# Up matmuls two tiles ahead of the down matmuls in three stretches of a routed feed-forward, attention, feed-forward kernel

## The reference

```python
x = L0_attn_x                                  # (32, 256, 128) float32, 8192 tokens of 128
x = x + 0.5 * ffn(layernorm(x), Wg, bg, W1, b1, W2, b2)
x = x + attn(layernorm(x), Wq, Wk, Wv, Wo)
x = x + 0.5 * ffn(layernorm(x), Wg, bg, W1, b1, W2, b2)

def ffn(x):                                    # 8 experts, hidden 512, the best 2 of each token
    probs, idx = top_k(softmax(x @ Wg + bg), 2)
    h = gelu(einsum('nd,edh->enh', x, W1) + b1)
    eo = einsum('enh,ehd->end', h, W2) + b2
    return einsum('nk,nkd->nd', probs, eo[idx])

def attn(x):                                   # 16 heads of 8 channels
    each token attends to itself and the 8 tokens before it
```

## Time and profile before

| what | value |
|---|---|
| median of 3 runs | 1040.05 us (1038.57 to 1041.2) |
| span of the profiled execution | 1184.4 us, 144.35 above the median; no other time of that execution is listed |
| PE busy | 883.4 us, 75% of the span |
| POOL busy | 665.5 us, 56% |
| DVE busy | 645.4 us, 54% |
| ACT busy | 501.1 us, 42% |
| mean granted clock of TensorE | 0.897 of full speed |

### The profile page before, as it was taken

The page is one execution under the profiler, slowest core; times in us unless marked ns, Lnnn a source line. Parts: engine busy times, 40 slices in busy tenths (PEclk is TensorE's granted clock), DMA queues, the critical chain, the costliest instruction groups (busy, mean ns, idle before and its releaser), DMA issues.

```text
span 1184.4 us, 22517 instructions
## 1 busy us (share of the span) xinstructions
PE 883.4 (75%) x6345; PEld 759.1 (64%) x6345; DVE 645.4 (54%) x1309; ACT 501.1 (42%) x1215; POOL 665.5 (56%) x593
## 2 busy tenths in 40 slices
PE   3347757576987789996999659897875766975983
PEld 3336647475866677785778545686765655864873
DVE  5774132431357688896989998686851411210222
ACT  4434424243623373744545325644342333422432
POOL 2574445545678666345677456356763545455552
PEclk9998859887989899998999978998986977987997
DMA  8314212262214421144112121422221224532683
GB/s 261 110 58 96 53 41 56 70 161 61 59 51 115 110 51 39 26 119 99 33 47 47 48 79 45 78 55 59 56 59 44 50 59 104 134 87 64 155 195 119
DMA packets 170488, 96.44 MB, mean 81 GB/s; under 512 B 137712, under 2 KB 154406, under 8 KB 169604
## 3 DMA queue, kind: packets, MB, share of 16 engines
q1 hardware_dynamic: 152420, 59.29, 21.7%
q0 software_dynamic: 17952, 35.71, 9.8%
HBM read 25.77 MB, written 52.35 MB: 66 GB/s over the span
## 4 chain that ended last, share of the span: by engine, by line
PE 40%; DVE 16%; issue 15%; another core or an unknown queue 14%; ACT 5%; DMA 4%; POOL 3%; SPq 3%; ACTq 0%; DVEq 0%; POOLq 0%
PE bank L979 16%; PE bank L962 11%; PE bank L877 3%; POOL x_sorted L591 3%; ACT h_f L766 2%; DVE prod L1167 2%; DVE prod L1178 2%; PE bank L850 2%; DMA x_sorted<-hl,slots_all 2%; DVE y_sb L1432 2%; PE bank L864 2%; PE bank L973 1%; DVE prod L1213 1%; PE bank L803 1%
## 5 line engine op out<-in xcount | busy, mean ns | idle before, releaser
L605 POOL DMA_INDIRECT y_pairs<-y_sb,tile_ids x305 | 355.1, 1164 | 329.5 <-issue 256.1
L766 ACT ACTIVATE h_f<-bank,b_cols 128x256 f32<-128x256 f32 (+1 forms) x736 | 266.0, 440 | 434.8 <-PE bank L962 242.6
L591 POOL DMA_INDIRECT x_sorted<-hl,slots_all x256 | 301.8, 1179 | 174.3 <-issue 87.0
L979 PE MATMUL bank<-w_sb,h_f 128*128 x2440 | 346.1, 295 | 20.8 <-issue 12.3
L979 PEld LDWEIGHTS bank<-w_sb,h_f 128*128 128x128 f32 x2440 | 317.6, 207 | 29.0 <-issue 24.7
L962 PE MATMUL bank<-xsT,w_hl 128*128 128x256 f16 (+1 forms) x2208 | 262.6, 269 | 59.1 <-ACT h_f L766 25.7
L962 PEld LDWEIGHTS bank<-xsT,w_hl 128*128 x2208 | 199.6, 104 | 97.1 <-issue 70.8
L1432 DVE TENSOR_TENSOR y_sb<-bank,tile_ids 128x256 f32<-128x256 f32 (+1 forms) x184 | 68.8, 375 | 328.5 <-PE bank L979 179.2
L973 PE MATMUL bank<-b_hl,ones_b 128*128 x184 | 49.8, 270 | 85.5 <-DVE y_sb L1432 69.7
L973 PEld LDWEIGHTS bank<-b_hl,ones_b 128*128 128x128 f16 x184 | 18.6, 101 | 104.7 <-issue 101.8
L1213 DVE TENSOR_TENSOR prod<-score,qkv 128x2304 f32<-128x2304 f32 x32 | 81.7, 2552 | 0.2
(11 more groups left out here) (159 smaller groups left out, 849.8 us busy)
## 6 DMA issues: line engine op xcount, KB each, us to landing
y_in<-y_pairs SPq DMA_DIRECT2D x28, 512.0 KB
x_sorted<-no_rows SPq DMA_DIRECT2D x7, 720.0 KB
y_pairs<-y_sb,tile_ids POOLq DMA_INDIRECT x305
x_sorted<-hl,slots_all POOLq DMA_INDIRECT x256
x_sorted<-no_rows SPq DMA_DIRECT2D x56, 72.0 KB
x_sb<-in_L_attn_x SPq DMA_DIRECT2D x3, 1024.0 KB, 6.4
out<-x_sb SPq DMA_DIRECT2D x3, 1024.0 KB
xsT<-x_sorted SPq DMA_TRANSPOSE x184
```

What stands on the lines that cost most here:

```text
L591: pool.indirect_dma_start(out=x_sorted[p], out_offset=bass.IndirectOffsetOnAxis(ap=slots_all[:, at:at + 1], axis=0), in_=hl[:, c % 2, i // ...
L605: pool.indirect_dma_start(out=y_pairs, out_offset=bass.IndirectOffsetOnAxis(ap=tile_ids[:, t.n % IDS, i, 0:1].bitcast(U32), axis=0), in_=y ...
L766: ins = act.activation(h_part(t, b)[:, k, :], bank[h_banks.uses[u][0]][:, k * t.slots:(k + 1) * t.slots], ACT.Gelu, bias=b1_cols[:, bass.d ...
L979: ins = pe.matmul(into[:, half, :], h_part(t, c // t.per)[:, c % t.per, half * P:(half + 1) * P], w2_flat[:, bass.ds((e * HC + c) * D, D)] ...
```

## The change

PE orders `up` and `down` anew in three stretches, banks are dealt anew, and group 3's turned tokens use one bank.

- The stages are cut elsewhere: stage 0 is part 0 and the first 8 tiles of part 1 (tiles 0 to 31), stage 2 begins at tile 24 of part 4 (tiles 120 to 183).
- In stages 0 and 2 `down` stands two tiles behind `up`; in stage 1 one tile, as before. At the end of a part all downs that are left come before the next part's first `up`.
- Up matmuls get bank 4 in stage 0 beside 0, 1 and 2, and tiles 120 to 159 go from banks (0, 1) to (0, 1, 2, 6). Down matmuls of tiles 120 to 159 go from bank 3 alone to (3, 7, 4), those of tiles 24 to 31 from bank 3 to (3, 7), and part 6 gets bank 4 as a third one.
- Since bank 4 is taken, all four quads of group 3 are turned in bank 5, each behind the copy of the one before.
- Two new waits on PE: tile 0 waits until the quads of groups 0 to 2 are copied, tile 120 until attention has been added in all groups and the last keys and values are copied.

```diff
+EARLY_END = (1, 8)
+LATE_BEGIN = (4, 24)
+AHEAD = (2, 1, 2)
@@ class Tile
-        self.stage = 0 if p == 0 else 2 if p == len(n_wide) - 1 else 1
+        self.stage = 0 if (p, at) < EARLY_END else 2 if (p, at) >= LATE_BEGIN else 1
+        self.ahead = AHEAD[self.stage]
@@ banks
-        h_banks, y_banks = Banks((0, 1, 2), (0, 1), (0, 1, 2, 6)), Banks((3, 7), (3,), (3, 7))
+        h_banks, y_banks = Banks((0, 1, 2, 4), (0, 1), (0, 1, 2, 6)), Banks((3, 7), (3,), (3, 7, 4))
+        def quad_bank(q, i):
+            return bank[5] if q == G - 1 else bank[4 + i % 2]
@@ ACT, copy_turned: reads quad_bank(q, i) in place of bank[4 + i % 2]
@@ PE, turn_quad
                 if n >= 2:
-                    pe.wait_ge(quads_ready, n - 1)
+                    pe.wait_ge(quads_ready, n if q == G - 1 else n - 1)
@@ PE, experts
-                earlier_tile = None
+                behind = []
                 for t in ALL_TILES:
-                    if t.begins_late:
-                        yield from down(*earlier_tile)
+                    while t.begins_late and behind:
+                        yield from down(*behind.pop(0))
...
                     e = of_these[t.at % LOADS]
+                    if t.n == 0:
+                        pe.wait_ge(quads_ready, (G - 1) * QUADS)
+                    if (t.p, t.at) == LATE_BEGIN:
+                        pe.wait_ge(attn_added, G * CH)
+                        pe.wait_ge(qkv_ready, G * KV)
                     yield from up(t, e)
-                    if earlier_tile and not t.begins_late:
-                        yield from down(*earlier_tile)
-                    earlier_tile = (t, e)
-                yield from down(*earlier_tile)
+                    behind.append((t, e))
+                    while len(behind) > t.ahead:
+                        yield from down(*behind.pop(0))
+                while behind:
+                    yield from down(*behind.pop(0))
```

More of the change, by code:

```diff
@@ L662, in copy_turned @@
                         act.wait_ge(quads_turned, q * QUADS + i + 1)
-                        act.copy(xnT_p[:, 4 * i:4 * i + 4, HALO:HALO + P], bank[4 + i % 2][:].rearrange("p (j n) -> p j n", n=P)
+                        act.copy(xnT_p[:, 4 * i:4 * i + 4, HALO:HALO + P], quad_bank(q, i)[:].rearrange("p (j n) -> p j n", n=P)
                                  ).then_inc(quads_ready, 1)
@@ L791, in turn_quad @@
                 if n >= 2:
-                    pe.wait_ge(quads_ready, n - 1)
+                    pe.wait_ge(quads_ready, n if q == G - 1 else n - 1)
                 for j in range(4):
-                    ins = pe.transpose(bank[4 + i % 2][:, j * P:(j + 1) * P], xn_at[q][:, 4 * i + j, :], ident[:])
+                    ins = pe.transpose(quad_bank(q, i)[:, j * P:(j + 1) * P], xn_at[q][:, 4 * i + j, :], ident[:])
                 ins.then_inc(quads_turned, 1)
```

## The result

The changed kernel takes **1047.0 us** (median of 7, 1044.16 to 1049.27), the kernel before beside it 1038.57 (median of 7, 1032.8 to 1042.1): ratio 1.008, 95% interval 1.0052 to 1.0108. It is slower by 0.8%, where 0.8% faster was forecast, and lies above the range's 1044. The granted clock isn't the difference: its mean over the seven runs is 0.931 of full speed for the changed kernel, and 0.931 over 26 runs of the kernel before.

The account below looks back on a forecast made before the run. No engine was full over the whole span; what counts is where PE, the busiest, is held. 1.6 + 0.6 - 1.7 - 4.1 - 3.2 - 1.0 = -7.8 us gave 1032, range 1022 to 1044.

Parts of the forecast that it names:

- Moved past: Stages 0 and 2: each `down` one `up` later (1.47 or 0.88 us) may delay DVE's `take_y`; counted 0.
- Starts of parts: PE at part starts: +1.1 and -1.2 us, cancelling for parts 5 and 6; +0.6 at tile 0, 0 for part 1.
- Rival 2: Slower: later results delay POOL's rows at parts 1 and 6, plus 1.1 at four starts; +6.1 us, 1046; chance 0.17.
- Waits taken away: PE's bank waits removed: part 1's head -1.7 us, part 4 -4.1, part 5 -3.2, part 6 -1.0.
- slowed stretches: Some 25 stretches of about 10 us with PE and SP slowed together, taken as profile recording, absent from timed runs.
- rival 1: POOL's scatters between results 135 and 153 hold part 6, so little changes: 1038 us; chance 0.33.
- Quads: Group 3's turned quads on PE: second waits for first's copy, 0.8 us for each of two pairs, +1.6.
- The new waits: PE's waits at tiles 0 and 120, for copies and additions expected to be done already: 0 us.
- Rival 3: Much faster: slowed stretches also occur in timed runs, a third of 69.7 us counts: 1018 us; chance 0.08.
- what would show it: Signs: PE's `y_sb` waits after tile 120 near 0 confirm banks; more PE idle before a part's first tiles refutes the forecast.

Follow-up runs that it names:

- a1: Changed kernel with `down` one tile behind `up` everywhere, keeping its banks, single quad bank and new waits; 1040.07 us, ratio 1.0005 to the kernel before.
- after: The changed kernel itself as profiled, against the kernel before; median 1047.0 us, ratio 1.008.
- b0: The kernel before, profiled a second time with no edit; one execution of 1043.77 us, span 1042.0, without slowed stretches.
- c1: a1 with SP's eight stores of zeros for parts 1, 5 and 6 issued behind eight earlier loads; 1036.15 us, ratio 0.998 to the kernel before.
- p1: Changed kernel with part 6's last 16 row scatters moved forward in POOL's table; 1047.07 us, ratio 1.0075 to the kernel before.
- c3: c1 with part 6's last four half steps of row scatters before results 142, 146, 149 and 152; 1024.76 us, ratio 0.9867 to the kernel before.

## Why the prediction was wrong

The forecast was -7.8 us and the measurement +8.4. By a1 and after the 16 us fall into two parts of similar size: the distance, forecast at about 0, costs 7 us (1040.07 to 1047.0), and the banks, forecast at 10 us of savings, save nothing measurable.

**"Moved past. ... I count 0"** is the step that failed by its mechanism. I had written that `take_y` and what is behind it may start later, and priced that at nothing because DVE is mostly idle. DVE's idleness was beside the point. Two chains hang on a result: POOL's scatters in table order, and SP, which waits for the scatter of eight tiles back. "xsT's loads are freed by `up`, not by `down`" holds for the buffer and not for the queue, in which an ids load that `down` frees stands ahead of the next `xsT` load (4.8 us for tile 133's, of the 6.8 in the trace after). That the distance costs is shown by the times; these paths are shown in the traces, and how they share the 7 us is not.

**Starts of parts, "0 for part 1", cancelling for 5 and 6.** I looked for the late load at a part's start (+1.1). In part 1 the expensive one comes later, at tile 29, where SP has put other loads between: 2.9 us more idle time after than in a1, a slower clock behind it, and one `down` still to do. Rival 2 had this form of loss, a `down` ready and put off behind a load, at a third of its price.

**Waits taken away, -9.0 in three terms.** Too large by the echo of the slowed stretches (b0: 0 for 1.7, 2.1 for 4.1, 1.1 for 6.4), and worth nothing measurable in time even where they went (a1). The -1.0 of part 6 fares no better: b0 has 0.2 us for ACT there (960 to 1035). The earlier trace rows lie between slowed stretches, and being outside one did not free them of it. For part 5, rival 1's reason is seen in c1's trace: POOL holds part 6.

**Quads, +1.6:** 1.59 in the trace, nothing that could be measured in the time. **The new waits, 0:** held. PE has none for `attn_added`.

**Rival 2** forecast 1046 and is nearest. The rows of part 1 do end later, at 171.9 instead of 169.1, 2.8 us where it had 0.9. But they barely set the start: by its list of waits SP stands there in b0 for its own stores (1.2 us), and after for the rows (0.7) and the stores (0.4), and tile 24's load leaves 1.8 us later. In part 6 the rows do set the start. Against b0 they aren't later (171.9 us from the end of attention to the last row scatter's end, 174.6 in b0), against a1 (166.6) they are by 5.3; one execution each. Its "+1.1 at four starts" was found at neither the place nor the size. So its sum is right in part by luck.

**Rival 3**'s sum doesn't come out as written: a third of 69.7 is 23 us, and with the -7.8 some 31 and not 22. It changes nothing, since timed runs are free of the stretches.

Of what would show it, I had named that PE's waits for `y_sb` vanish and that its idle time before loads grows. The first fell from 34.1 to 27.3 over the span, and to nothing from 800 to 852 us; the second grew from 50.1 to 61.9.

## What to carry to other kernels

Putting a consumer step one item later is free only if nothing that feeds the producer waits for it. Follow its result through every queue back to the loads, and look for each place where the producer waits for a load: there the step put off was what filled the wait. And where a stage starts behind two chains, ask what shortening one does to the other. Moving POOL's rows forward held back SP's last load, and the stores of zeros behind that load then came last: nothing gained on the changed kernel (p1). With the stores moved first, which alone gave 0.2%, too little to be sure of, moving the rows by a milder table gave 1.3% in all. That the table alone would not have done it is an estimate, not a run.

## What was not expected of the hardware

POOL's scatters take 0.96 us (rows) or 0.98 us (results) at the median and mostly have 0.30 between them, 1.26 or 1.29 us from one to the next; one in twenty takes over 2.4 us. In runs of them POOL can take no more though its busy share reads 77%, and its 64% of the span hid that its last row scatter set the start of part 6: the load of tile 160 leaves SP 2.1 us behind that scatter's end in b0, after, a1, c1 and c3 alike. A burst of four row scatters is followed by 2.1 to 4.5 us of waiting for it to land when nothing stands between (b0, after, c1), and by none when five results do (c3). And of two profiled executions of one program, one spanned 142 us more than the other.
